# Q, K and V of batches 1 to 7 as three one-pass float32r products of 12-bit parts, made by GpSimd, in fills of 512 columns

## The chip, the cores and the metric

The kernel runs on one core of a Trainium2 chip. The metric is the device time of one execution in microseconds, the median of several runs. The engines are TensorE (PE in the profile, its weight loads PEld), VectorE (DVE), ScalarE (ACT), GpSimd (POOL) and SyncE (SP), which issues most of the DMAs.

## The reference, cut to what matters

The input x has 8 sequences ("batches" below) of 1,024 tokens and 256 features. One attention block with 16 heads of 16 dimensions is followed by two groups of a mixture of experts. Everything is float32.

```python
q = (x @ Wq.T + bq).reshape(B, L, H, Dh)
k = (x @ Wk.T + bk).reshape(B, L, H, Dh)
v = (x @ Wv.T + bv).reshape(B, L, H, Dh)
q = _rope(q, sin, cos)
k = _rope(k, sin, cos)
scores = jnp.einsum('bqhd,bkhd->bhqk', q, k) / jnp.sqrt(jnp.float32(Dh))
attn = jax.nn.softmax(scores, axis=-1)
out = jnp.einsum('bhqk,bkhd->bqhd', attn, v).reshape(B, L, D)
x = _layernorm(x + (out @ Wo.T + bo))
...
# two groups of 32 experts, top 2 of each, SwiGLU with 128 hidden units
x = _layernorm(x + moe(x))
```

The change touches the first three lines only (and where their results and the rotation's are kept).

## The kernel before

**Steps.** The attention of all eight batches is one software pipeline of 512 steps, 64 for a batch. A unit is four heads of a batch and takes 16 steps. In each step t TensorE does four score matmuls of 512 columns for the softmax maxima, 22 steps ahead (line 990, into two banks `ps_a` that VectorE reduces, two TENSOR_REDUCE a step on line 1242), four transposed score matmuls of 512 columns (line 980, into a ring of three banks `ps_b` that ScalarE turns into probabilities, four ACTIVATE a step on line 845), and the products of probabilities and V of step t-2 (line 1009, four heads side by side in the array). A score of line 990 and one of line 980 lie on different halves of the array's rows and go as a pair.

**Jobs.** Other work of TensorE is hung on steps by `schedule` and `chain_at`. For a batch that begins at step `start`, Q is computed in 8 steps and K in 8 (a block c of 128 output features and a quarter of 256 tokens each, line 908), and V in 8 (128 tokens each, line 918). They are float32 matmuls, two for a fill, one for each 128 input features. The steps of batch b carry the jobs for batch b+1. Counted from the start of a batch, Q and K stand in steps 8 to 15 and 31 to 38, and V in 57 to 63 and in step 0 of the next. The output projection of the batch before (O) has steps 22 to 29, the transposes (T) and the router (L) steps 48 to 53, the counts (R) step 14, and the rows of maxima (M) steps 12, 28, 44 and 60.

**Product with V, whole or halved.** It goes in two halves of 256 columns, between the score pairs, only where a step has no job:

```python
if in_a and 0 < (t - PV_LAG) % KC < KC - 1 and not b_jobs.get(t) and not a_jobs.get(t):
    pv(t - PV_LAG, k * HALF // 2, (k + 1) * HALF // 2)
elif k == 0:
    pv(t - PV_LAG, 0, HALF)
```

**VectorE's chores.** Layer norm, top 2, routing and ranks are cut into pieces that `between(t)` puts behind the reductions of a step, as far as a `room` reaches. In batches 0 to 6, room is 7 in a step with Q, K or V, 5 with O, and 0 in any other. Pieces of kind 0 (the split of the maxima, and `split_upper`, the masks that cut Q and K to their upper 12 bits) go out at their step whatever the room.

**GpSimd** works through `pool_order`: `split` (rotation of Q and K, six operations on 128 by 1,024 elements, then `lower`, two subtractions), `norm_o`, `choose`, `rank_sums`, and `list`, whose four scatters each wait for a given step of the product with V. SP sends out the parts of Q and K (`parts_out`), reads them back in stacked form (`stack`), and loads the next x (`next_x`) in one piece of 1 MB. All of these queues are in order. After the steps comes the expert stage, which the change leaves as it is but for a name.

## Time and profile before

| what | value |
|---|---|
| median of 3 runs | 2279.51 us (2279.37 to 2288.64) |
| span of the profiled execution | 2348.8 us |
| attention steps 0 to 63 (batch 0) | 182.8 us |
| attention steps 192 to 255 (batch 3) | 200.9 us |
| busy in batch 3: PE, DVE, ACT, POOL | 197.05, 177.88, 157.79, 92.82 us |
| first to last maximum of scores | 33.8 to 1611.4 us |

A step is read as the time from the start of its first TENSOR_REDUCE of line 1242 to that of the next step's; a batch has 128 of them. Busy times are sums over the stretch, and a busy TensorE isn't TensorE at its peak: the records overlap, so costs are taken from the starts of matmuls. The profiled execution is longer than the timed ones, so that differences are worked out against its own span.

### The profile page before, as it was taken

The page shows a single profiled execution, that of the slowest core. Times are in us where ns is not written, and L with a number is a line of the kernel's source. Part 1 is how long each engine was busy: PE and PEld are TensorE (multiplying, and loading weights), DVE is VectorE, ACT ScalarE, POOL GpSimd, SP SyncE. Part 2 cuts the span into 40 slices and gives each one's busy share as a digit, 9 for nine tenths or more (in the row PEclk, how much of TensorE's full clock was granted, in tenths as well). Part 3 has the DMA queues.
Part 4 walks back from the last instruction along what each step waited for, and adds up shares of the span by engine and source line. Part 5 has one row for each costly group of instructions (what it writes and reads, how often), then busy time and mean ns, then how long its engine had stood idle before and what let it go on. Part 6 is the DMA issues. An engine that isn't in the chain of part 4 may idle for free.

```text
span 2348.8 us, 46747 instructions
## 1 busy us (share of the span) xinstructions
PE 2205.4 (94%) x13885; PEld 1125.7 (48%) x13893; DVE 1774.4 (76%) x3301; ACT 1599.4 (68%) x3621; POOL 1037.2 (44%) x886
## 2 busy tenths in 40 slices
PE   8999999999999999999999999999888888999994
PEld 4433343433433343344344344333476666777773
...
GB/s 178 91 87 90 122 95 53 132 109 116 160 117 95 140 155 114 118 144 134 85 161 150 103 123 141 185 125 191 190 164 167 135 182 226 226 330 298 285 272 204
DMA packets 179667, 363.70 MB, mean 155 GB/s; under 512 B 31009, under 2 KB 113185, under 8 KB 175329
## 3 DMA queue, kind: packets, MB, share of 16 engines
...
## 4 chain that ended last, share of the span: by engine, by line
PE 78%; DVE 11%; issue 4%; ACT 2%; DMA 1%; another core or an unknown queue 1%; POOL 1%; SPq 1%; ACTq 0%; DVEq 0%; POOLq 0%
PE ps_a L990 24%; PE ps_o L1009 20%; PE ps_a L1797 7%; DVE maxima_sb L1242 7%; PE ps_b L908 5%; PE ps_b L1821 4%; PE ps_b L1797 3%; PE ps_b L980 3%; PE ps_b L918 3%; PE ps_a L1784 3%; PE ps_o L1821 2%; PE ps_b L1806 2%; ACT probs_sb L845 1%; PE ps_b L928 1%
## 5 line engine op out<-in xcount | busy, mean ns | idle before, releaser
L1242 DVE TENSOR_REDUCE maxima_sb<-ps_a 128x1 f32<-128x1024 f32 x1024 | 1233.8, 1220 | 184.1 <-PE ps_a L990 164.4
L845 ACT ACTIVATE probs_sb<-ps_b 128x512 f32<-128x512 f32 x2013 | 1087.2, 600 | 283.7 <-PE ps_b L980 244.3
L990 PE MATMUL ps_a<-k_stack_sb,q_stack_sb 48*128 48x512 f32 x2048 | 736.4, 444 | 25.6 <-DVE maxima_sb L1242 23.8
L980 PE MATMUL ps_b<-q_stack_sb,k_stack_sb 50*128 50x512 f32 x2013 | 745.3, 450 | 4.2 <-ACT probs_sb L845 2.6
L1009 PE MATMUL ps_o<-probs_sb,v_sb_sb 128*32 128x512 f32 (+1 forms) x5400 | 586.7, 507 | 0.7 <-ACT probs_sb L845 0.5
L990 PEld LDWEIGHTS ps_a<-k_stack_sb,q_stack_sb 48*128 48x128 f32 x2048 | 304.8, 185 | 552.5 <-issue 281.5
L1648 POOL DMA_INDIRECT y_dram<-y_rows_sb,spot_sb x318 | 313.5, 986 | 258.1 <-DVE y_rows_sb L2110 107.9
L174 POOL DMA_INDIRECT rows_dram<-stage_sb,listed_sb x208 | 202.6, 974 | 306.1 <-PE ps_o L1009 280.4
L980 PEld LDWEIGHTS ps_b<-q_stack_sb,k_stack_sb 50*128 50x128 f32 x2013 | 305.5, 186 | 47.5 <-ACT probs_sb L845 39.2
L1797 PE MATMUL ps_a<-w_gu_sb,x_cols_sb 128*128 x848 | 226.1, 390 | 4.5 <-ACT x_cols_sb L1704 2.8
L1009 PEld LDWEIGHTS ps_o<-probs_sb,v_sb_sb 128*32 128x32 f32 x5400 | 106.6, 108 | 236.1 <-issue 107.7
L414 POOL TENSOR_TENSOR feat_qk_sb<-feat_qk_sb,trig_sb 128x1024 f32<-128x1024 f32 x30 | 71.3, 2376 | 283.0 <-DMA swapped_sb<-feat_qk_sb 209.1
L1704 ACT ACTIVATE x_cols_sb<-ps_a 128x256 f32<-128x256 f32 x318 | 123.1, 388 | 99.4 <-PE ps_a L1784 49.1
L2101 DVE TENSOR_TENSOR spot_sb<-x_rows_sb,spare_sb 128x1 int32<-128x1 f32 x237 | 37.7, 159 | 175.9 <-ACT gate_sb L1710 108.3
L1797 PEld LDWEIGHTS ps_a<-w_gu_sb,x_cols_sb 128*128 128x128 f32 x848 | 149.1, 195 | 19.9 <-issue 7.2
L1821 PE MATMUL ps_b<-w_d_sb,hidden_t_sb 128*128 x416 | 135.0, 407 | 17.5 <-DVE y_rows_sb L2110 12.8
L1710 ACT ACTIVATE gate_sb<-ps_a 128x128 f32<-128x128 f32 x212 | 59.9, 283 | 123.4 <-PE ps_a L1797 69.1
L1784 PE MATMUL ps_a<-consts_sb,x_rows_sb 128*128 128x128 f32 x636 | 124.0, 277 | 3.6 <-DMA x_rows_sb<-rows_dram 3.6
L1806 PE MATMUL ps_b<-consts_sb,hidden_sb 128*128 128x128 f32 x318 | 89.5, 282 | 33.9 <-ACT hidden_t_sb L1755 16.8
L1797 PE MATMUL ps_b<-w_gu_sb,x_cols_sb 128*128 x424 | 111.6, 386 | 2.3 <-ACT x_cols_sb L1704 2.1
L1784 PEld LDWEIGHTS ps_a<-consts_sb,x_rows_sb 128*128 128x128 f32 x636 | 90.1, 143 | 39.9 <-issue 5.4
L808 ACT ACTIVATE feat_qk_sb<-ps_b,bias_sb 128x256 f32<-128x256 f32 x128 | 60.8, 475 | 68.1 <-PE ps_b L908 65.2
...
## 6 DMA issues: line engine op xcount, KB each, us to landing
...
```

The lines of the kernel that those rows point to most:

```text
L174: return pool.indirect_dma_start(dram["rows"][g], bass.IndirectOffsetOnAxis(ap=index, axis=0), source, None)
L845: act.activation(probs[t % NPR][:, j, :], src[:, :], ACT.Exp, scale=float(DH) ** -0.5).then_inc(s_bdrain, 1)
L980: pe.matmul(out[:, :], k_stack[u % NSTK][lo:lo + XROWS, jj, kc * P:(kc + 1) * P].bitcast(F32R), q_stack[u % NSTK][lo:lo + XROWS, jj, qh * ...
L990: ins = pe.matmul(out[:, kh, :], q_stack[u % NSTK][lo:lo + ROWS, jj, qt * P:(qt + 1) * P].bitcast(F32R), k_stack[u % NSTK][lo:lo + ROWS, j ...
L1009: ins = pe.matmul(ps_o[32 * j:32 * j + 32, lo:hi], v[:, at:at + 32], probs[t % NPR][:, j, lo:hi], start=kc == 0, stop=kc == KC - 1)
L1242: vec.tensor_reduce(maxima[u % 2][:, 1 - k, i:i + 1], src[:, :, :].rearrange("p a q -> p (a q)"), AX.X, ALU.max).then_inc(s_adrain, 1)
L1648: pool.indirect_dma_start(dram["y"][n // NT], bass.IndirectOffsetOnAxis(ap=spot[n % NSP][:, :], axis=0), y_rows[n % NY][:, :], None).then_ ...
L1704: act.activation(x_cols[n % NXT][:, :, :], ps_x[n % 2][:, 0:DC, :], ACT.Copy).then_inc(s_xc, 1)
L1784: ins = pe.transpose(ps_x[n % 2][:, dc, :], x_rows[n % NXG][:, dc * P:(dc + 1) * P], con("ident"))
L1797: ins = pe.matmul(ps_g[n % NGU][:, 0:2 * HID], x_cols[n % NXT][:, dc, :], w_gu[g][:, bass.ds(e * (DC * 2 * HID) + dc * 2 * HID, 2 * HID)], ...
L1806: pe.transpose(ps_h[:, 0:P], hidden[n % NGU][:, :], con("ident")).then_inc(s_ht, 1)
L1821: pe.matmul(y_bank(n)[:, 0:D], hidden_t[n % 2][:, :], w_d[:, bass.ds(e * D + down_at(g), D)], start=True, stop=True).then_inc(s_down, 1)
```

## The change

For batches 1 to 7, x and the weights are cut into an upper part, rounded by a copy into float32r, and a lower part, the rest. The product is then three float32r matmuls for each 128 input features: upper by upper, lower x by upper w, upper x by lower w. Q and K are filled 512 columns at a time, in four phases (block c, half h of the tokens), and V two blocks of 128 tokens at a time, so that 24 jobs become 12. In steps of the batch before they stand at 7, 9, 16, 18, 36, 38, 49 and 51 (Q and K) and at 40, 42, 58 and 62 (V). x arrives in halves of 512 KB, four loads for a batch, and GpSimd splits each (`x_split`). The masks of VectorE are gone; GpSimd makes both parts of Q and K (`part`, a copy and a subtraction). Q and K no longer have a tile of their own but lie in the lower part's place, so ScalarE waits for the parts of the block before to be out in DRAM before it writes them. The chain of norm, transposes and routing moves by some steps, ScalarE scales two blocks of rows a step in place of one, and VectorE's room is set anew.

```diff
+        else:
+            for c in range(DC):
+                for h in range(2):
+                    at = start + PHASE_AT[2 * c + h]
+                    put(b_jobs, at, "Q", b, c, h)
+                    put(b_jobs, at + 2, "K", b, c, h)
+                    if c == 1:
+                        for i, v in enumerate(V_AT[h]):
+                            put(b_jobs, start + v, "V", b, 2 * h + i)
...
-        at = dict(O=22, norm=23, scale=39, T=48, L=50, x1=48, top2=57, exp=67, route=73, choose=74, marks=75, R=78, ranks=79,
-                  rank_sums=80, choices=86)
+        at = dict(O=22, norm=23, scale=40, T=44, L=46, x1=44, top2=50, exp=73, route=74, choose=75, marks=76, R=78, ranks=79,
+                  rank_sums=80, choices=85)
...
+PRODUCTS = ((0, 0), (0, 1), (1, 0))
...
+PHASE_AT, V_AT = (-57, -48, -28, -15), ((-24, -22), (-6, -2))
+X_AT, X_SPLIT_AT = (-65.5, -54, -45, -21), (-61, -51, -37, -18)
...
-        k_step = lambda b, c: SPB * b + (-48, -16)[c]
-        pool_order = []
+        k_step = lambda b, c: SPB * b + ((-45, -12) if b else (-48, -16))[c]
...
+        def part(eng, b, c, which):
+
+            n = b * DC + c
+            at = pool_no[("split", (b, c))] + 6 + 2 * which
...
+            eng.wait_ge(s_pool, at)
+            eng.tensor_copy(parts[which][:, 0, :].bitcast(F32R), feat[which]).then_inc(s_pool, 1)
+            eng.wait_ge(s_pool, at + 1)
+            eng.tensor_tensor(feat[which], feat[which], parts[which][:, 0, :], ALU.subtract).then_inc(s_pool, 1)
+
+        def x_split(eng, b, phase):
+
+            n = x_no(b, phase)
+            eng.wait_ge(s_xt, 16 * (n + 1))
+            eng.tensor_copy(x_parts[:, 0], x_in).then_inc(s_xupper, 1)
+            eng.wait_ge(s_xupper, n + 1)
+            eng.tensor_tensor(x_parts[:, 1], x_in, x_parts[:, 0].bitcast(F32), ALU.subtract).then_inc(s_xlower, 1)
...
                 if q == 0 and (b, c) != (0, 0):
-                    wait_split(act, b * DC + c - 1)
...
+                    act.wait_ge(s_parts, 16 * 2 * (b * DC + c))
...
-                    i, n = t - at["scale"], 1 if at["rate"] == 1 else 4
+                    i, n = t - at["scale"], 2 if at["rate"] == 1 else 4
...
+            def features(which, b, c, h):
+                out = b_tile()
+                pe.wait_ge(s_wparts, 2)
+                pe.wait_ge(s_xlower, x_no(b, 2 * c + h) + 1)
+                for n, (dc, w, x) in enumerate((dc, w, x) for dc in range(DC) for w, x in PRODUCTS):
+                    ins = pe.matmul(out[:, :], (w_upper, w_lower)[w][:, which, dc, c * P:(c + 1) * P],
+                                    x_parts[:, x, dc, :], start=n == 0, stop=n == DC * len(PRODUCTS) - 1)
+                ins.then_inc(s_bfill, 1)
+
+            def values(b, i):
+                out = b_tile()
+                pe.wait_ge(s_xlower, x_no(b, 2 + i // 2) + 1)
+                for a in range(2):
...
-                        chores += [(at, 0, split_upper(b, c, 0)), (at + 3, 0, split_upper(b, c, 1))]
...
+                    room[0] = min(room[0], 0) + 6
+                elif any(name in held for name in "QKV"):
+                    room[0] = min(room[0], 0) + 14
                 else:
-                    room = 7 if any(name in held for name in "QKV") else 0
+                    room[0] = min(room[0], 0) + (5 if "T" in held else 2)
```

On TensorE, in the steps before a batch begins, a V fill (`ps_b<-w_v_sb,x_t_sb`) has two matmuls. Before:

```order
L990 MATMUL ps_a<-k_stack_sb,q_stack_sb 128x512
L980 MATMUL ps_b<-q_stack_sb,k_stack_sb 128x512
L918 MATMUL ps_b<-w_v_sb,x_t_sb 128x256 x2
L990 MATMUL ps_a<-k_stack_sb,q_stack_sb 128x512
L980 MATMUL ps_b<-q_stack_sb,k_stack_sb 128x512
```

Now, for batch 1, lines 1068 and 1058 being the former 990 and 980:

```order
L1068 MATMUL ps_a<-k_stack_sb,q_stack_sb 128x512
L1058 MATMUL ps_b<-q_stack_sb,k_stack_sb 128x512
L996 MATMUL ps_b<-w_upper_sb,x_parts_sb 128x256 x2
L996 MATMUL ps_b<-w_lower_sb,x_parts_sb 128x256
L996 MATMUL ps_b<-w_upper_sb,x_parts_sb 128x256 x2
L996 MATMUL ps_b<-w_lower_sb,x_parts_sb 128x256
L996 MATMUL ps_b<-w_upper_sb,x_parts_sb 128x256 x2
L996 MATMUL ps_b<-w_lower_sb,x_parts_sb 128x256
L996 MATMUL ps_b<-w_upper_sb,x_parts_sb 128x256 x2
L996 MATMUL ps_b<-w_lower_sb,x_parts_sb 128x256
L1068 MATMUL ps_a<-k_stack_sb,q_stack_sb 128x512
```

Twelve matmuls for 256 tokens stand where two stood for 128. A fill of Q or K is six matmuls of 512 columns in the same way.

On GpSimd, early in a batch's steps, between `norm_o` (`o_feat_sb`) and `rank_sums` (`totals_sb`), before:

```order
L468 TENSOR_TENSOR o_feat_sb<-o_feat_sb,o_den_sb 128x1024
L470 TENSOR_SCALAR o_feat_sb<-o_feat_sb,bias_sb 128x1024
L497 TENSOR_TENSOR totals_sb<-incl_sb,totals_sb 128x512
L499 TENSOR_TENSOR totals_sb<-totals_sb,counts_sb 128x512
```

and now:

```order
L514 TENSOR_TENSOR o_feat_sb<-o_feat_sb,o_den_sb 128x1024
L516 TENSOR_SCALAR o_feat_sb<-o_feat_sb,bias_sb 128x1024
L477 CAST x_parts_sb<-x_t_sb 128x1024
L479 TENSOR_TENSOR x_parts_sb<-x_t_sb,x_parts_sb 128x1024
L543 TENSOR_TENSOR totals_sb<-incl_sb,totals_sb 128x512
L545 TENSOR_TENSOR totals_sb<-totals_sb,counts_sb 128x512
```

The second half of x is split behind `norm_o`, and TensorE needs it in step 16.

On VectorE, around steps 8 to 15 of a batch (`maxima_sb` the reductions, two a step), the same pieces stand in both programs; before they lie in steps that hold Q or K, now only step 9 does. Now:

```order
L1320 TENSOR_REDUCE maxima_sb<-ps_a 128x1 x2
L1177 RECIPROCAL den_sb<-den_sb 128x128
L1320 TENSOR_REDUCE maxima_sb<-ps_a 128x1 x4
L1168 TENSOR_SCALAR max_parts_sb<-maxima_sb 128x2x16
L1171 TENSOR_TENSOR max_parts_sb<-maxima_sb,max_parts_sb 128x2x16
L1217 TENSOR_REDUCE denom_sb<-shifted_sb 128x16
L1220 RECIPROCAL denom_sb<-denom_sb 128x16
L1320 TENSOR_REDUCE maxima_sb<-ps_a 128x1 x4
L1227 TENSOR_TENSOR hot_sb<-consts_sb,expert_sb 128x512 x2
L1320 TENSOR_REDUCE maxima_sb<-ps_a 128x1 x4
L1156 COPY totals_sb<-ps_a 128x2x8x32
L1158 COPY logits_sb<-ps_a 128x512
```

A count of x4 is two steps without a chore between them.

## Rows read from the trace of the kernel before

**Rows 1.** The page: busy time of the engines, and the chain of waits by engine

```profile
PE 2205.4 (94%) x13885; PEld 1125.7 (48%) x13893; DVE 1774.4 (76%) x3301; ACT 1599.4 (68%) x3621; POOL 1037.2 (44%) x886
...
PE 78%; DVE 11%; issue 4%; ACT 2%; DMA 1%; another core or an unknown queue 1%; POOL 1%; SPq 1%; ACTq 0%; DVEq 0%; POOLq 0%
```

**Rows 2.** Busy time by stretch, batch 0 and batch 3

```profile
core 0: us, PE busy (x) PEld busy (x) DVE busy (x) ACT busy (x) POOL busy (x), PEclk, DMA share, GB/s
88.80:271.70 182.90, 181.46 (x1336) 71.62 (x1338) 157.91 (x141) 151.85 (x292) 42.42 (x17) 1.00 0.40 97
672.60:873.50 200.90, 197.05 (x1363) 81.50 (x1360) 177.88 (x244) 157.79 (x306) 92.82 (x71) 1.00 0.47 128
```

**Rows 3.** Timeline of PE, half of a step without a job

```profile
686.04 0.64 PE L1009 MATMUL ps_o<-probs_sb,v_sb_sb 128*32 128x256 f32 x8
686.61 0.50 PE L990 MATMUL ps_a<-k_stack_sb,q_stack_sb 48*128 48x512 f32 x1
...
686.94 0.39 PE L990 MATMUL ps_a<-k_stack_sb,q_stack_sb 48*128 48x512 f32 x1
...
687.27 0.64 PE L1009 MATMUL ps_o<-probs_sb,v_sb_sb 128*32 128x256 f32 x8
```

**Rows 4.** Timeline of PE around a Q job (start, length)

```profile
778.43 1.13 PE L908 MATMUL ps_b<-x_t_sb,w_q_sb 128*128 128x256 f32 x4
779.49 0.50 PE L990 MATMUL ps_a<-k_stack_sb,q_stack_sb 48*128 48x512 f32 x1
...
779.83 0.39 PE L990 MATMUL ps_a<-k_stack_sb,q_stack_sb 48*128 48x512 f32 x1
...
780.16 1.07 PE L1009 MATMUL ps_o<-probs_sb,v_sb_sb 128*32 128x512 f32 x8
781.15 0.50 PE L990 MATMUL ps_a<-k_stack_sb,q_stack_sb 48*128 48x512 f32 x1
```

**Rows 5.** Timeline of weight loads, the same Q job

```profile
778.43 0.73 PEld L908 LDWEIGHTS ps_b<-x_t_sb,w_q_sb 128*128 128x128 f32 x4 [0.36 <-issue]
```

**Rows 6.** The chain of waits in order of time, a router job of 64 columns

```profile
426.47 0.84 PE ps_a L952 x8
```

**Rows 7.** Busy by stretch: steps 8-15 and 16-21 of batch 3, 8-15 of batch 7

```profile
693.50:722.90 29.40, 28.99 (x174) 12.28 (x177) 24.85 (x28) 22.27 (x44) 11.25 (x8) 1.00 0.32 85
722.90:737.60 14.70, 14.45 (x124) 5.14 (x126) 14.12 (x13) 12.54 (x25) 13.68 (x9) 1.00 0.60 111
...
1500.90:1525.30 24.40, 21.53 (x174) 7.42 (x170) 24.15 (x27) 18.75 (x36) 11.88 (x9) 1.00 0.53 160
```

**Rows 8.** Timeline of DVE, a step without a job and with a chore

```profile
1505.07 0.68 DVE L1139 TENSOR_REDUCE denom_sb<-shifted_sb 128x16 f32<-128x512 f32 x1
1505.66 2.35 DVE L1242 TENSOR_REDUCE maxima_sb<-ps_a 128x1 f32<-128x1024 f32 x2
1507.92 0.17 DVE L1086 TENSOR_SCALAR max_parts_sb<-maxima_sb 128x32 int32<-128x32 int32 x1
```

**Rows 9.** Busy by stretch, the masks of line 439 alone, batch 3

```profile
672.60:873.50 200.90, 3.50 (x4) 1.00 0.47 128
```

**Rows 10.** Timeline of POOL: last scatter before norm_o, norm_o, rank_sums

```profile
688.22 0.97 POOL L174 DMA_INDIRECT rows_dram<-stage_sb,listed_sb  x1 [1.49 <-PE ps_o L1009]
...
708.65 2.37 POOL L468 TENSOR_TENSOR o_feat_sb<-o_feat_sb,o_den_sb 128x1024 f32<-128x1024 f32 x1 [6.97 <-DMA o_den_sb<-inv_dram]
...
716.42 2.85 POOL L470 TENSOR_SCALAR o_feat_sb<-o_feat_sb,bias_sb 128x1024 f32<-128x1024 f32 x1
```

**Rows 11.** Groups by line and form, POOL (busy us, mean ns)

```profile
L747 POOL MEMSET v_sb_sb<- 128x2192 f32 x1 | 1.9, 1930 | 0.1
```

**Rows 12.** Timeline of ACT, a step in which it also scales a block

```profile
799.15 0.60 ACT L869 ACTIVATE y_sb<-y_sb,shift_sb,rstd_sb 128x256 f32<-128x256 f32 x1
799.65 2.08 ACT L845 ACTIVATE probs_sb<-ps_b 128x512 f32<-128x512 f32 x4
801.62 0.60 ACT L869 ACTIVATE y_sb<-y_sb,shift_sb,rstd_sb 128x256 f32<-128x256 f32 x1
```

**Rows 13.** Timeline of SP: rows for the lists, parts out, stacks in

```profile
772.38 0.36 SPq L672 DMA_DIRECT2D stage_sb<-x_dram  x1
772.84 0.41 SPq L586 DMA_DIRECT2D parts_dram<-parts_k_sb  x1
778.52 1.79 SPq L610 DMA_DIRECT2D q_stack_sb<-parts_dram  x4
```

More of the change, by code:

```diff
@@ L386, in program @@
             pool_no[(name, args)] = count
-            count += {"split": SPLIT_STEPS if args != (0, 0) else 0, "bias_y": 1, "norm_o": 2 * DC, "choose": 0, "rank_sums": 0, "list": 0}[name]
+            count += {"split": SPLIT_STEPS if args != (0, 0) else 0, "bias_y": 1, "norm_o": 2 * DC, "choose": 0, "rank_sums": 0, "list": 0,
+                      "x_parts": 0, "w_parts": 0}[name]
         norm_o_done = lambda b: pool_no[("norm_o", (b,))] + 2 * DC
@@ L410, in rotate @@
             f = feat[which]
-            eng.wait_ge(s_bdrain, b_no[("QK"[which], b, c, QUARTERS - 1)] + 1)
+            eng.wait_ge(s_bdrain, b_no[("QK"[which], b, c, pieces(b) - 1)] + 1)
             wait_swapped(eng, b, c, which)
@@ L417, in rotate @@
             eng.tensor_tensor(f[:, :], f[:, :], swapped, ALU.add).then_inc(s_pool, 1)
-        def lower(eng, b, c, which):
+        def part(eng, b, c, which):
             n = b * DC + c
-            eng.wait_ge(s_mask, 2 * n + which + 1)
-            if n:
-                eng.wait_ge(s_parts, 16 * 2 * n)
+            at = pool_no[("split", (b, c))] + 6 + 2 * which
+            if which == 0 and c == 1 and b >= 2:
+                eng.wait_ge(s_afill, a_no[("L", b - 2, KC // 2 - 1)] + 1)
+            eng.wait_ge(s_parts, 16 * 2 * n)
@@ L559, in swap @@
             def swap(b, c, which):
-                sp.wait_ge(s_bdrain, b_no[("QK"[which], b, c, QUARTERS - 1)] + 1)
+                sp.wait_ge(s_bdrain, b_no[("QK"[which], b, c, pieces(b) - 1)] + 1)
                 if which == 1:
@@ L761, in attention_gpsimd @@
                     rotate(pool, *args, 1)
-                    lower(pool, *args, 0)
-                    lower(pool, *args, 1)
+                    part(pool, *args, 0)
+                    part(pool, *args, 1)
+                elif name == "x_parts":
+                    x_split(pool, *args)
+                elif name == "w_parts":
+                    w_split(pool)
                 elif name == "bias_y":
@@ L951, in route @@
                     for dc in range(DC):
-                        ins = pe.matmul(out[:, 0, a * NG * NE:(a + 1) * NG * NE], x1_of(b)[:, 2 * i + a, dc, :], router[:, dc, :],
+                        ins = pe.matmul(out[:, 0, a * NG * NE:(a + 1) * NG * NE], x1_of(b, 2 * i + a)[:, dc, :], router[:, dc, :],
                                         start=dc == 0, stop=dc == DC - 1)
@@ L1091, in split_max @@
                 yield 2
-            def split_upper(b, c, which):
-                upper(vec, b, c, which)
-                yield 4
             def recip(b):
@@ L1193, in attention_vector @@
                     at = chain_at(nb, b)
[L1194 to L1195 removed]
+                    chores += [(end + 8, 0, recip(b)), (at["norm"], 2, norm(b)), (at["top2"], 3, top2(b)), (at["route"], 0, route(b)),
+                               (at["marks"], 0, marks(b)), (at["ranks"], 0, ranks(b)), (at["choices"], 0, ranks_of_choices(b))]
             chores.append((chain_at(nb, nb - 2)["table"], 7, early_table()))
+            room = [0]
             def between(t):
```

148 lines of the change are left out of this document (88 added, 60 removed).

## The prediction

> **What bounds the kernel now.** I read the page first. TensorE is busy 94% of the span and holds 78% of the chain of waits, with VectorE at 11% [rows 1]. A busy TensorE says little by itself, so I went to the stretches. A batch from the second on costs some 200 us: in batch 3 TensorE is busy 197.05 of 200.9 us, VectorE 177.88, ScalarE 157.79, GpSimd 92.82, all at a granted clock of 1.00, the 2.4 GHz level; batch 0 is shorter and has little of VectorE's chores [rows 2]. Then the timeline, to price a step by the starts of its matmuls. In a step without a job two pairs of scores take 0.33 us each and half the product with V 0.57 us (686.04 to 686.61 to 686.94 to 687.27), in all 1.23 us a half and 2.46 a step [rows 3]. With a job, the product with V is whole and takes 0.99 us (780.16 to 781.15), and the pairs 4 x 0.33, which makes 2.31 us, and the job adds 778.43 to 779.49, 1.06 us: 3.37 us in all [rows 4]. VectorE is close behind: two reductions back to back take 2.26 us (1505.66 to 1507.92) of those 2.46 [rows 8], so a step without a job has 0.2 us for chores and one with a job 1.1. ScalarE fills a step to the end once it also scales a block: 801.62 - 799.15 = 2.47 us for five instructions, 0.49 each [rows 12]. The reader should see three engines within 10% of each other in the empty steps. TensorE work that is saved in a batch moves time only as far as the other two let it.
>
> **TensorE's part.** Removed are 24 job steps of a batch at 3.37 us, 80.9 us. Added are 12 job steps, and 12 become empty at 2.46 us, 29.5 us (an empty step is dearer than 2.31 since its product with V is halved). The price of a new job isn't in the trace. The old job has four records, each 256 columns in two passes, 512 clocks, and its weight loads lie behind the matmul ahead, as four loads spread over 0.73 us show [rows 5]. Four times 0.213 us leaves 0.21 us for entry and exit of 1.06. A float32r matmul of 512 columns in one pass is again 512 clocks, so six give 6 x 0.213 + 0.21 = 1.49 us. The bound above is that each one pays what a pair of scores pays, 0.33 us [rows 3], that is 1.98. I take 1.49, since the shape is that of the old job: full array, no switch of tiles. For V, twelve matmuls of 256 columns are 12 x 0.107 + 0.21 = 1.49 us if the load of 128 columns hides. The router's eight loads come 0.84/8 = 0.105 us apart [rows 6], just as long as such a matmul, so it is close; in series they would give 12 x 0.212 = 2.5. I take 1.59. New sum: 8 x 3.80 + 4 x 3.90 + 29.5 = 75.5 us, so **-5.4 us a batch**; at the upper bounds (+3.9 and +3.6) it would be +2.1.
>
> The Trainium skill, "TensorE: Matmul & The Clock Gate", section "Back-to-back issue gap", gives about 131 ns for a sustained matmul of 512 columns in a real kernel. By it, as an estimate, a Q or K job would be 1.0 us and the change worth 27 us more over seven batches. The rows here don't agree: no quarter of the job of 1.06 us can be that short, and I leave it out of the sum.
>
> **VectorE's part.** The masks go, 3.50 us a batch [rows 9]. Two lay in O steps and two in V steps, partly covered; I take **-1.0**. But the chores stay, and half of the steps with room for them lose their job. The last batch shows what that costs, since it has the same chores and no projections: its steps 8 to 15 take 24.4 us with VectorE busy 24.15, against 29.4 in batch 3 [rows 7]. The K job in step 9 adds some 0.9 of its 1.34 us, so 25.3, a saving of 4.1 where TensorE's price alone (seven steps at -0.91, one at +0.43) says 5.9: **+1.8** back. In step 21, now an empty one, stand two reductions of the kind on line 1139 (0.68 us each [rows 8]) and a small one, 1.5 us; with 0.2 us of room a step and a bank of lag, **+0.8**. The single small pieces that the new room of 2 lets into empty steps fit in the 0.2.
>
> **ScalarE.** In steps 40 to 43 it has 16 probabilities, 8 scalings, 2 V drains and a copy of o, 27 x 0.49 = 13.2 us, where TensorE has 2 x 3.90 + 2 x 2.46 = 12.7. **+0.3**, as the old scaling steps had a part of this too. Larger drains (8 of 512 for 16 of 256) save ScalarE time that nobody waits for.
>
> **GpSimd.** Four x splits and the copies of `part` are new: eight copies and four subtractions of 1,024 elements. The subtraction is 2.37 us as other two-input operations are [rows 10]. A copy lies between the memset, 1.93 us for 2,192 elements or 0.9 for 1,024 [rows 11], and the operation with a scalar, 2.85 us [rows 10]; I take 1.1, since a copy has no arithmetic. Together 18 us on a queue that is busy 93 of 201 us: not a bound, but it is in order and TensorE now waits for it. First split: the last scatter ends at 689.2, 16.6 us into the batch [rows 10], or 15.8 by the new step times; 3.6 us more is 19.4, and TensorE comes to the Q of step 7 at 7 x 2.46 + 2.31 = 19.5. No wait. Second: `norm_o` ends at 719.27 [rows 10], 46.7 us in, and the split 50.3. TensorE gets to step 16's job at 17.2 + 3.8 + 25.3 + 2.3 = 48.6: it waits, **+1.5**. A wait here holds up all that is queued behind on TensorE, so both other engines starve. At 2.85 a copy these waits would be 1.7 and 3.5 us, +3.7 for the batch. The fourth split, ahead of step 49, has two steps of cover, some 6 us for 4.6.
>
> The Trainium skill, "GPSIMD Engine Reference", section "4.1 Engine selection", would leave elementwise work with VectorE, GpSimd being about twice as slow on two inputs and about line rate on one. For the subtraction the trace agrees (2.37 us); for the copy it would mean an estimate of 0.9 us, and a sum lower by 0.2 us a wait.
>
> **DMA.** The x halves carry the bytes of before. `parts_out` of the first block now stands on SP behind the rows for the third list, whose wait for a scatter ended at 772.38, 99.8 us in [rows 13]. One step later is 102.3. Both parts then go out together; 1 MB alone needed 5.7 us before the stack could be issued (772.84 to 778.52), two may need up to 11.4. They land 108.7 to 114.4 us in, and ScalarE, which now waits for them before it writes Q, gets there at about 114. Cost nothing, just.
>
> **Sum.** -5.4 - 1.0 + 1.8 + 0.8 + 0.3 + 1.5 = -2.0 us a batch. Six batches (1 to 6): -12. Batch 0 has neither O nor ranks, so -5.4 and -0.8 for its masks: -6.2. Batch 7 loses the V of its step 0, -0.9. In all -19 us: 2348.8 becomes 2330 in the profiled execution. The timed runs have a median 69 us below that span; attention ran at full clock in the profile, so I put the same 19 us on the median: **2260 us**.
>
> **Rivals.**
> 1. Half of TensorE's gain eaten, as worked out: 2248 to 2268, chance 0.50.
> 2. TensorE's whole gain arrives, because the lag of banks covers the chores and GpSimd is early: 7 x -6.4 = -45, 2235. For it: VectorE has 23 us a batch to spare. Against: steps 8 to 15 of the last batch. Chance 0.12.
> 3. All of it is eaten, by VectorE's chores and the second split with a dear copy: -2.0 + 2.2 = about 0 a batch, -5 in all, 2274. Chance 0.24.
> 4. Slower, by one mechanism: the parts of the first block land late and ScalarE stands in step 36 with the probabilities queued behind it, so that the three banks fill and TensorE stops. It costs each us beyond 114. From 5 us late on, in six batches, the kernel is slower than before by over 0.5%; at 8 us it is 2279.5 - 19 + 48 = 2308. For it: the order on SP and a margin of about nothing. Against: 5.7 us for 1 MB. Chance 0.11. Weight loads in series and pairs' price (+7.5 a batch, 2312) have 0.03.
>
> **How the numbers follow.** The likeliest is the first, its own range 2248 to 2268. The range for 8 in 10 takes in most of 2 and 3: 2238 to 2284. About 0.5%, 11 us, is what a measurement of this kernel can tell from no change. Faster by more: the first two, 0.62; within: the third, 0.24; slower: the fourth and the series of loads, 0.14.
>
> **What would show it.** A Q fill should take 1.5 us from its first matmul to the next score, a V fill 1.5 to 1.7; steps 8 to 15 of a middle batch about 25 us; a wait of TensorE for GpSimd's lower x ahead of the second Q fill, 1 to 2 us a batch, and none ahead of the others; the cast on GpSimd 0.9 to 1.5 us; batch 0 about 176.5 us and batch 3 about 199. I am wrong if float32r pays more than a pass, if the cast costs over 2 us, or if ScalarE waits for the parts' DMA.

## The result and the profile after

The changed kernel takes **2341.06 us** (median of 4 runs, 2326.39 to 2350.82); the kernel before, on the same chip, 2279.44 us (2278.08 to 2288.64). The ratio is 1.0247, 95% interval 1.0191 to 1.0303: slower by 2.5%. I had forecast 2260, with 0.62 on faster. Comparisons leave disturbed runs out, so a ratio can differ a little from that of two medians.

The page of the changed kernel, busy time by engine and the chain by engine:

```profile
PE 2199.2 (94%) x14349; PEld 1143.9 (49%) x14357; DVE 1775.5 (76%) x3271; ACT 1580.9 (67%) x3537; POOL 1171.8 (50%) x974
...
PE 70%; DVE 14%; issue 4%; POOL 3%; ACT 3%; DMA 3%; SPq 2%; ACTq 0%; DVEq 0%; POOLq 0%
```

Against [rows 1] TensorE's busy time hardly moved, and its share of the chain fell from 78 to 70%: what came in its place is VectorE, GpSimd and transfers. VectorE lost its masks and has the same busy time, 1775.5 for 1774.4. That is the first sign that something else in it grew.

Busy time by stretch: 33 to 120 us, batch 0, batches 1 to 6 together, batch 3, and its steps 8 to 15 and 16 to 21 (us, then PE, PEld, DVE, ACT, POOL busy with counts, the granted clock, DMA):

```profile
33.00:120.00 87.00, 86.74 (x215) 43.80 (x213) 59.71 (x53) 14.45 (x31) 28.63 (x14) 0.51 0.36 96
108.60:295.00 186.40, 183.23 (x1404) 74.84 (x1406) 158.03 (x136) 148.33 (x281) 65.07 (x31) 0.96 0.39 88
295.00:1552.10 1257.10, 1190.55 (x8548) 501.22 (x8556) 1065.39 (x1406) 928.40 (x1758) 621.33 (x441) 0.98 0.47 124
710.20:915.70 205.50, 194.33 (x1427) 82.24 (x1426) 176.75 (x239) 154.72 (x294) 112.01 (x84) 1.00 0.49 131
731.90:759.30 27.40, 24.22 (x182) 9.03 (x178) 25.60 (x26) 19.83 (x38) 13.95 (x10) 1.00 0.31 93
759.30:779.90 20.60, 18.07 (x134) 7.33 (x132) 16.37 (x17) 15.04 (x28) 11.22 (x9) 1.00 0.62 126
```

Batch 3 against [rows 2]: TensorE's busy time fell by 2.7 us, as it should, but the batch grew by 4.6, so TensorE stands idle 11.2 us where it stood 3.9. Steps 8 to 15 take 27.4 us against 29.4 [rows 7]; I had said 25.3. The clock is the 2.4 GHz level all through batch 3. In the stretch from 33 to 120 us it is at half, with TensorE busy without a gap, and 0.98 over batches 1 to 6.

The kernel before, profiled once more (e4), gives the yardstick that the first profile could not: its stretch behind the last maximum of the scores is 669 us, where the first profile had 739. The same stretches of it (33 to 120 us, batches 1 to 6, batch 3):

```profile
33.00:120.00 87.00, 83.02 (x376) 38.32 (x377) 77.61 (x70) 31.29 (x63) 18.74 (x8) 0.96 0.41 110
...
274.50:1481.80 1207.30, 1182.72 (x8157) 489.77 (x8164) 1063.18 (x1443) 946.13 (x1830) 510.01 (x369) 1.00 0.46 123
677.30:878.10 200.80, 196.99 (x1363) 81.62 (x1360) 177.72 (x243) 157.68 (x306) 92.69 (x71) 1.00 0.46 128
```

The spans differ by 2349.0 - 2274.8 = 74.2 us. Of these 49.8 are in batches 1 to 6 (1257.1 - 1207.3), 17.8 ahead of step 0 (108.6 against 90.8), 2.6 in batch 0, 4 behind. So there are two questions: what costs 8.3 us a batch, and what halves the clock in the prelude.

**The jobs cost what I had said.** Timeline of PE, the Q fill in step 7 of batch 3, the first of batch 4's projections:

```profile
729.54 0.70 PE L986 MATMUL ps_b<-x_parts_sb,w_upper_sb 128*128 128x512 f32 x2
730.08 0.40 PE L986 MATMUL ps_b<-x_parts_sb,w_lower_sb 128*128 128x512 f32 x1
730.31 0.62 PE L986 MATMUL ps_b<-x_parts_sb,w_upper_sb 128*128 128x512 f32 x2
730.77 0.40 PE L986 MATMUL ps_b<-x_parts_sb,w_lower_sb 128*128 128x512 f32 x1
731.10 0.50 PE L1068 MATMUL ps_a<-k_stack_sb,q_stack_sb 48*128 48x512 f32 x1
```

731.10 - 729.54 = 1.56 us (predicted 1.49); a V fill took 1.62 (1.59). The Q fill of step 16 had to wait first:

```profile
761.69 0.70 PE L986 MATMUL ps_b<-x_parts_sb,w_upper_sb 128*128 128x512 f32 x2 [2.16 <-POOL x_parts_sb L479]
```

**What I had not looked for** stands in the timelines of DVE and POOL around step 12 of batch 3, first DVE:

```profile
747.01 2.43 DVE L1227 TENSOR_TENSOR hot_sb<-consts_sb,expert_sb 128x512 bf16<-128x512 f32 x2
749.36 2.34 DVE L1320 TENSOR_REDUCE maxima_sb<-ps_a 128x1 f32<-128x1024 f32 x2
...
758.02 1.38 DVE L1237 TENSOR_TENSOR_SCAN incl_sb<-scan_bf_sb,totals_sb 128x512 f32<-128x512 bf16 x1
```

and POOL:

```profile
745.88 2.40 POOL L514 TENSOR_TENSOR o_feat_sb<-o_feat_sb,o_den_sb 128x1024 f32<-128x1024 f32 x1 [2.58 <-DMA o_den_sb<-inv_dram]
748.38 3.69 POOL L516 TENSOR_SCALAR o_feat_sb<-o_feat_sb,bias_sb 128x1024 f32<-128x1024 f32 x1
752.05 2.36 POOL L514 TENSOR_TENSOR o_feat_sb<-o_feat_sb,o_den_sb 128x1024 f32<-128x1024 f32 x1
754.50 2.84 POOL L516 TENSOR_SCALAR o_feat_sb<-o_feat_sb,bias_sb 128x1024 f32<-128x1024 f32 x1
757.29 1.03 POOL L477 CAST x_parts_sb<-x_t_sb 128x1024 fp32r<-128x1024 f32 x1
758.41 3.13 POOL L479 TENSOR_TENSOR x_parts_sb<-x_t_sb,x_parts_sb 128x1024 fp32r<-128x1024 f32 x1
```

The two one-hot tables take 2.43 us, where the kernel before needs 1.36. The first of them takes 1.82 us for 0.68 and ends at 748.83, 0.55 us behind GpSimd's operation (748.28). GpSimd's next one, begun at 748.38 beside the rest of the tables, takes 3.69 instead of 2.85. Each engine pays for the other. At 758.41 the split of x meets the scan, and takes 3.13 us instead of 2.38. The maxima, which read PSUM and run through all of this, keep their 1.22.

One line's instructions in batches 1 to 6, of before (e4) (min/median/max in ns): the split of the maxima, the tables, the scan, the list positions

```profile
L1086 DVE TENSOR_SCALAR max_parts_sb<-maxima_sb x24: 170/171/172, 305.1 to 1463.6; 128x32 int32<-128x32 int32 x24
L1149 DVE TENSOR_TENSOR hot_sb<-consts_sb,expert_sb x10: 680/682/685, 507.6 to 1315.4; 128x512 bf16<-128x512 f32 x10
L1159 DVE TENSOR_TENSOR_SCAN incl_sb<-scan_bf_sb,totals_sb x5: 1197/1202/1225, 522.9 to 1330.1; 128x512 f32<-128x512 bf16 x5
L1181 DVE SCALAR_TENSOR_TENSOR listed_sb<-expert_sb,rank_sb x5: 176/178/180, 551.8 to 1357.8; 128x32 int32<-128x32 f32 x5
```

and of the changed kernel, with the maxima as a control:

```profile
L1168 DVE TENSOR_SCALAR max_parts_sb<-maxima_sb x24: 170/174/2384, 325.8 to 1536.0; 128x32 int32<-128x32 int32 x24
L1227 DVE TENSOR_TENSOR hot_sb<-consts_sb,expert_sb x10: 677/1248/2854, 536.9 to 1375.7; 128x512 bf16<-128x512 f32 x10
L1237 DVE TENSOR_TENSOR_SCAN incl_sb<-scan_bf_sb,totals_sb x5: 1384/2439/2524, 547.9 to 1386.3; 128x512 f32<-128x512 bf16 x5
L1259 DVE SCALAR_TENSOR_TENSOR listed_sb<-expert_sb,rank_sb x5: 561/775/820, 570.6 to 1405.9; 128x32 int32<-128x32 f32 x5
L1320 DVE TENSOR_REDUCE maxima_sb<-ps_a x770: 1159/1224/1227, 293.8 to 1552.1; 128x1 f32<-128x1024 f32 x193
```

The same code, up to 14 times as long in its worst instance. The Trainium skill names this: "SBUF — State Buffer", section "SBUF: two separate sides", says that VectorE in a two-port mode, or with two inputs in SBUF (against a GpSimd instruction that reads SBUF), and GpSimd take one pair of ports as an exclusive lock for a whole instruction, and the other waits; the trace agrees (2384 ns for 170).

Call an instruction's duration less the shortest of the same form in that trace its stretched time. Summed over VectorE's instructions that lost over 0.1 us, reductions left out (they vary by 0.07 us with or without GpSimd), it is 26.1 us in batches 1 to 6, against 6.2 before. To it come TensorE's waits for the lower x parts, 9.9 us in four (5.38 in batch 1, 2.17 and 2.16 in batches 2 and 3, and 0.15), and the clock: 58.0 us of batches 1 to 6 at the 1.2 GHz level against 3.4, in pieces of 3.4 to 10.2 us, which begin during or just behind a wait of TensorE for the one or the other (batch 3, all at 2.4 GHz, was an exception).

### The profile page after: what moved, and what is told of

It reads as the page before. It is cut to its first block, busy times and chain, and to the rows that moved or that the text cites. A ratio compares the mean times of both kernels' runs of the same rounds, so it can differ in the third digit from the quotient of the medians.

```text
span 2349.0 us, 47558 instructions
## 1 busy us (share of the span) xinstructions
PE 2199.2 (94%) x14349; PEld 1143.9 (49%) x14357; DVE 1775.5 (76%) x3271; ACT 1580.9 (67%) x3537; POOL 1171.8 (50%) x974
## 3 DMA queue, kind: packets, MB, share of 16 engines
q10 hardware_dynamic: 1464, 2.38, 0.4%
## 4 chain that ended last, share of the span: by engine, by line
PE 70%; DVE 14%; issue 4%; POOL 3%; ACT 3%; DMA 3%; SPq 2%; ACTq 0%; DVEq 0%; POOLq 0%
PE ps_a L1068 20%; PE ps_o L1087 18%; DVE maxima_sb L1320 8%; PE ps_a L1875 6%; PE ps_b L1899 3%; PE ps_b L1875 3%; PE ps_b L986 3%; PE ps_b L1058 3%; PE ps_a L1862 2%; PE ps_o L1899 2%; PE ps_b L996 2%; ACT probs_sb L906 1%; PE ps_b L1884 1%; PE ps_b L967 1%; SPq L577 1%
## 5 line engine op out<-in xcount | busy, mean ns | idle before, releaser
L1068 PE MATMUL ps_a<-k_stack_sb,q_stack_sb 48*128 48x512 f32 x2048 | 746.1, 460 | 46.6 <-DVE maxima_sb L1320 42.2
L1058 PE MATMUL ps_b<-q_stack_sb,k_stack_sb 50*128 50x512 f32 x2013 | 762.1, 456 | 8.2 <-ACT probs_sb L906 6.1
L1087 PE MATMUL ps_o<-probs_sb,v_sb_sb 128*32 128x256 f32 (+1 forms) x5864 | 604.3, 484 | 1.1 <-ACT probs_sb L906 0.5
L1068 PEld LDWEIGHTS ps_a<-k_stack_sb,q_stack_sb 48*128 48x128 f32 x2048 | 315.8, 193 | 555.8 <-DVE maxima_sb L1320 404.6
L1058 PEld LDWEIGHTS ps_b<-q_stack_sb,k_stack_sb 50*128 50x128 f32 x2013 | 311.1, 188 | 65.9 <-ACT probs_sb L906 58.5
L1087 PEld LDWEIGHTS ps_o<-probs_sb,v_sb_sb 128*32 128x32 f32 x5864 | 115.9, 108 | 256.9 <-issue 168.0
L1875 PE MATMUL ps_a<-w_gu_sb,x_cols_sb 128*128 x848 | 221.2, 384 | 0.7 <-ACT x_cols_sb L1782 0.7
L1899 PE MATMUL ps_b<-w_d_sb,hidden_t_sb 128*128 x416 | 129.8, 394 | 8.6 <-DVE y_rows_sb L2188 5.4
L454 POOL TENSOR_TENSOR parts_q_sb<-parts_q_sb,trig_sb 128x1024 f32<-128x1024 f32 x15 | 35.7, 2378 | 177.1 <-DMA swapped_sb<-parts_q_sb 177.0
L1833 ACT ACTIVATE hidden_t_sb<-ps_b 128x128 f32<-128x128 f32 x318 | 88.0, 277 | 4.7 <-PE ps_b L1884 4.5
```

Source lines behind the costliest of these rows:

```text
L1058: pe.matmul(out[:, :], k_stack[u % NSTK][lo:lo + XROWS, jj, kc * P:(kc + 1) * P].bitcast(F32R), q_stack[u % NSTK][lo:lo + XROWS, jj, qh * ...
L1068: ins = pe.matmul(out[:, kh, :], q_stack[u % NSTK][lo:lo + ROWS, jj, qt * P:(qt + 1) * P].bitcast(F32R), k_stack[u % NSTK][lo:lo + ROWS, j ...
L1087: ins = pe.matmul(ps_o[32 * j:32 * j + 32, lo:hi], v[:, at:at + 32], probs[t % NPR][:, j, lo:hi], start=kc == 0, stop=kc == KC - 1)
L1875: ins = pe.matmul(ps_g[n % NGU][:, 0:2 * HID], x_cols[n % NXT][:, dc, :], w_gu[g][:, bass.ds(e * (DC * 2 * HID) + dc * 2 * HID, 2 * HID)], ...
L1899: pe.matmul(y_bank(n)[:, 0:D], hidden_t[n % 2][:, :], w_d[:, bass.ds(e * D + down_at(g), D)], start=True, stop=True).then_inc(s_down, 1)
```

## The experiments

All twelve in one table. "Batches 1-6" is the length of that stretch in the windows view (its ends are the first maximum of step 0 of batches 1 and 7); "low" is the time in it at the 1.2 GHz level; "stretched" is worked out as above. All in us.

| kernel | median | ratio to before (95%) | batches 1-6 | low | stretched |
|---|---|---|---|---|---|
| before again (e4) | 2276.7 (one run) | | 1207.3 | 3.4 | 6.2 |
| changed | 2341.06 | 1.0247 (1.0191-1.0303) | 1257.1 | 58.0 | 26.1 |
| e1 more unread | 2337.86 | 1.0247 (1.0162-1.0332) | 1247.1 | 37.5 | 24.6 |
| e2 256 columns | 2354.35 | 1.0325 (1.0273-1.0376) | 1268.2 | 85.3 | 32.2 |
| e3 plain float32 | 2350.69 | 1.0286 (1.0238-1.0334) | 1257.5 | 37.5 | 21.1 |
| e5 x early | 2307.89 | 1.0090 (1.0053-1.0127) | 1222.2 | 17.1 | 16.1 |
| e6 and tables alone | 2302.42 | 1.0098 (1.0056-1.0140) | 1222.4 | 20.5 | 14.9 |
| e7 fills over chores | 2348.76 | 1.0259 (1.0176-1.0343) | 1261.0 | 71.7 | 28.1 |
| e8 parts on GpSimd only | 2315.22 | 1.0122 (1.0072-1.0171) | 1238.6 | 47.8 | 28.1 |
| e9 e6 and three waits | 2302.50 | 1.0055 (1.0020-1.0090) | 1220.2 | 17.1 | 8.1 |
| e10 e8 and one wait | 2278.14 | 0.9984 (0.9946-1.0023) | 1204.6 | 0 | 6.9 |
| e12 e9, a wait moved | 2289.62 | 1.0021 (0.9982-1.0059) | 1210.9 | 10.2 | 1.5 |
| e11 e12, scaling spread | 2277.33 | 0.9977 (0.9937-1.0016) | 1199.3 | 0 | 0.6 |

### e1 and e4: is it the clock of the prelude?

```diff
-UNREAD = 19
+UNREAD = 21
```

> The changed kernel with 21 instead of 19 of the unread matmuls of the prelude, nothing else. Theory A (the clock of the first 120 us): in the changed kernel's profile TensorE waits 1.8 us for the first stack behind the last unread matmul, and the granted clock is 0.5 from 33.5 us for 85 us; two more unread matmuls at 0.4 us each fill half of that wait, so the low stretch should be gone and the time should fall by about 20 us, to 2321. Rival: the fall of the clock has another cause than this gap; then the stretch from 33.5 us stays and the time stays at 2341.

> The kernel before, profiled once more. Its first profile had a span of 2349 us though its timed runs took 2279, and its stretch behind the last attention step (1610 us on) took 739 us against 670 in the changed kernel. If that is a matter of the one execution, this profile has a tail near 670 us, and a span near 2280; if it belongs to every profiled execution, it is 739 us again.

In e1 TensorE goes into the first score without the gap of 1.8 us, and the clock falls all the same, 5 us later (38.5 us on, for 78.5), with no gain in time. Theory A falls. Later profiles settle more: e6 and e12, with the whole change in them, kept the clock up over most of the prelude (step 0 at 90.0 and 89.8 us), e6 even behind a gap of 2.36 us, and so did e10 behind one of 2.48. e8, whose prelude differs from that of before in a copy for a mask, did not.

The runs of the kernel before form two groups: of the 23 timed beside e11 and e12, 12 take 2268.98 to 2286.93 us at a mean granted clock of 0.982 to 0.990, and 11 take 2289.82 to 2300.90 at 0.969 to 0.976. The means of the groups differ by 18 us, as much as the fall cost in the prelude (17.8). So the fall of the prelude's clock seems to happen to the kernel before as well (inferred: neither of its two profiles caught one), and the change isn't needed for it. Whether the change makes it more frequent stays open.

It bears on the size of the loss: the four runs of before beside the changed kernel (2278.08 to 2288.64) look like the first group, while the changed kernel's profile has the fall; its fastest run, 2326.39, is 47 us above the median before. e4 shows that the 739 us tail was a matter of one execution.

### e2 and e3: fill size, and the price of the products

e2 gives each phase four fills of 256 columns, in 24 steps; e3 keeps the 12 fills and takes the parts away.

```diff
# e2
-                    put(b_jobs, at, "Q", b, c, h)
-                    put(b_jobs, at + 2, "K", b, c, h)
+                    for i in range(2):
+                        put(b_jobs, at + i, "Q", b, c, 2 * h + i)
+                        put(b_jobs, at + 2 + i, "K", b, c, 2 * h + i)
...
# e3
-                for n, (dc, w, x) in enumerate((dc, w, x) for dc in range(DC) for w, x in PRODUCTS):
+                for dc in range(DC):
+                    ins = pe.matmul(out[:, :], (w_q, w_k)[which][:, dc, c * P:(c + 1) * P], x_in[:, dc, :],
...
```

> The changed kernel with the size of a fill undone: 24 fills of 256 columns a batch (8 for each of Q, K, V) in 24 steps, still of three float32r products of the parts that GpSimd makes. The steps between them are given to VectorE's chores as before the change (8 a step). Theory B (VectorE's chores lie bare, since 12 of the 24 steps that covered them are now empty): the steps with a fill are about 3.2 us instead of 3.37 before and cover the chores again, so a batch is about 200 us instead of 205 to 215, and the time about 2290 or less. Rival C (the extra work on GpSimd, or the wait for its x parts, is what costs): little changes, 2325 to 2345.

> The changed kernel with its 12 fills of 512 columns a batch in their 12 steps, but of plain float32 matmuls (2 a fill) straight from x; GpSimd splits neither x nor the weights. A fill should take about 1.9 us instead of 1.56. Theory B (chores bare in empty steps): the 12 jobs cost 12 x 0.35 = 4 us more a batch, the wait for GpSimd's x parts (2 us in the batch looked at) goes, so about 2341 + 7 x 2 = 2355 us. Rival C (GpSimd's splits and what they hold up are the loss): a batch is 3 us or more shorter in spite of the longer fills, 2320 or less.

e2 is slower still. The fills are short (a step of 3.22 us), and there are 24 steps to cover chores again, yet nothing comes back. This isn't a clean test of theory B, since three other things grew: the stretched time (32.2) and the low clock (85.3), the highest of all, and a new wait. With Q of the second block in step 37, ScalarE waits there for the parts' transfer (19.4 us in batches 2 to 6), and TensorE behind it for 11.5:

```profile
ACT parts_q_sb L869 <- DMA parts_dram<-parts_k_sb: 19.4, 5, 6.9
PE ps_b L1060 <- ACT parts_q_sb L869: 11.5, 5, 5.3
```

(us in total, times, longest.) That is the mechanism of my rival 4. e3 meets the number of theory B, 2351 for 2355, but says little by it: longer fills raised TensorE's work, and the stretched time fell only from 26.1 to 21.1. The copies of `part` and the later placement were still there, which I take for the reason; no run separates them.

### e5 and e6: GpSimd's order in steps 11 to 15

```diff
-X_AT, X_SPLIT_AT = (-65.5, -54, -45, -21), (-61, -51, -37, -18)
+X_AT, X_SPLIT_AT = (-65.5, -54.9, -45, -21), (-61, -52.75, -37, -18)
-                pool_order.append((SPB * (b + 1) + 11, "norm_o", (b,)))
+                pool_order.append((SPB * (b + 1) + 11.5, "norm_o", (b,)))
# e6 also, in norm_o
+            if 1 <= b < nb - 1:
+                eng.wait_ge(s_route, ROUTE_STEPS * b)
```

> The changed kernel with the second split of x on GpSimd ahead of the normalisation of the attention output instead of behind it (its load one step earlier), nothing else. Theory D (TensorE's wait for x parts is 2.2 us of the 5 to 6 us that a batch is longer than before): the wait of the second Q fill goes, an undisturbed batch is 203.8 us instead of 206.0, and the time about 15 us lower, 2325. Rival: the wait was hidden behind VectorE's chores in the same steps, so something else is late next (the ranks at step 14 to 21), a batch stays at 206 and the time at 2340.

> The kernel of e5 with, in addition, a wait of GpSimd's normalisation until VectorE has made its two one-hot tables at step 12. Theory E (VectorE's operations with two SBUF inputs, or narrow copies from SBUF to SBUF, don't start or don't end while GpSimd runs an operation: in the changed kernel the two tables take 2.6 us or more instead of 1.37, the scan 2.0 instead of 1.2, the splits of the maxima up to 2.4 instead of 0.17, 28 us in all over seven batches against 6 before the change): here the two tables run beside the x split at worst, step 12 is about 1 us shorter than in e5, and the sum of such stretched time falls from 28 us to about 20. Rival: the stretched rows are not on TensorE's path; then the rows get shorter and the batch doesn't.

e5 takes 33 us off the median, twice the 15 that I expected. TensorE's waits for x parts fall from 9.9 to 0.3 us; with them go 10 us of stretched time (the tables and the scan no longer meet anything long) and 41 us of low clock. A wait costs more than its length when the clock falls behind it. Batch 3 itself moved only from 205.5 to 205.0, with a low piece of 3.4 us in it. I had expected e6 to make step 12 a microsecond shorter than in e5. That was a miss: step 12 of batch 3 is 3.78 us in e6 and 3.79 in e5 (4.93 in the changed kernel), so the earlier split had already kept GpSimd off the tables. The list positions of step 21 and the splits of step 26 stay stretched in both (steps of 4.50 and 5.14 us in e6), and batches 1 to 6 stay at 1222: no gain over e5 that these runs can tell.

### e7: fills over the longest chores

```diff
-PHASE_AT, V_AT = (-57, -48, -28, -15), ((-24, -22), (-6, -2))
-X_AT, X_SPLIT_AT = (-65.5, -54, -45, -21), (-61, -51, -37, -18)
+PHASE_AT, K_AFTER, V_AT = (-57, -47, -27, -15), (5, 4, 2, 2), ((-23, -21), (-6, -2))
+X_AT, X_SPLIT_AT = (-65.5, -51.9, -42.5, -20.5), (-61, -51, -35, -18)
...
```

> The changed kernel with four of the twelve fills moved so that they stand in the steps with VectorE's longest chores (K of the first half to step 12, beside the one-hot tables; Q and K of the second half to steps 17 and 21, beside the rank reductions), what hangs on them a step or three later, and a little more room for chores in the other steps. Theory B (in a step without a fill VectorE's own two maxima, 2 x 1.22 us, are as long as the step, so that each chore there is bare, and in a step with a fill up to 1.5 us of chores is covered): steps 12 and 21 together are 9.3 us in the changed kernel and about 2.5 us of that falls away, 15 us over the program, to 2325. Rival: what is taken off there comes back as a wait for x parts at step 17 or for the parts at step 37, 2340 or more.

A miss. Step 12 took 6.00 us in batches 2, 3 and 5, its tables stretched by 2.21, and 4.23 in batch 4, where they weren't. At step 33 a split of x now met VectorE's Newton chain (the inverse root of layer norm) and stretched it by 2.7 us. The rival that I had named came true as well: with Q of the second block in step 37, ScalarE waited for the parts, and TensorE for ScalarE, batches 1 to 6:

```profile
ACT parts_q_sb L868 <- DMA parts_dram<-parts_k_sb: 22.0, 5, 8.0
PE ps_b L1058 <- ACT parts_q_sb L868: 13.5, 4, 6.3
```

The x waits fell from 9.9 to 3.0 us in return. To move a fill moves GpSimd and the transfers behind it, so this run doesn't settle theory B either.

### e8 and e10: one part of the change, and one wait

e8 is the kernel before, with `upper` on GpSimd as a copy to float32r. e10 adds one wait ahead of the addition of the bias to y.

```diff
# e8
-                    lower(pool, *args, 0)
-                    lower(pool, *args, 1)
+                    for which in range(2):
+                        upper(pool, *args, which)
+                        lower(pool, *args, which)
...
-                        chores += [(at, 0, split_upper(b, c, 0)), (at + 3, 0, split_upper(b, c, 1))]
# e10 also
                     pool.wait_ge(s_y, 16 * (b + 1))
+                    if b < nb - 1:
+                        pool.wait_ge(s_max, MAX_STEPS * (UPB * (b + 1) + 1))
```

> The kernel before with only one part of the change: GpSimd makes the upper parts of Q and K (a copy to float32r, 1.04 us) instead of VectorE (a mask, 0.68 us, four a batch); fills, x and placement as before. Theory E (GpSimd and VectorE hold each other up): the four masks of 0.68 to 2.7 us go from VectorE, which by themselves cost before at most 6 us over the program in stretched time; GpSimd's rows move little, so the time is 2270 to 2280: this part alone is not what made the kernel slower. Rival: the 1.04 us copies behind each rotation stretch VectorE's other rows or delay the stacks, 2290 or more.

> The kernel of e8 (before, with only the upper parts of Q and K made on GpSimd) with one wait more: GpSimd's addition of the bias to y (4.57 us) waits until VectorE has split the maxima at step 58. In e8 that split waited 3.9 us for the addition in each batch, step 58 took 7.40 us instead of 3.28, and the clock fell behind it. Theory E: step 58 is 3.3 us again, the clock stays up in steps 60 to 62, a batch is 200 us or less, and the time 2270 to 2280. Rival: the 4.1 us go elsewhere (another row of VectorE meets the later addition), and the time stays at 2300 or more.

My number for e8 was wrong, and its rival right: 2315. Timeline of DVE in e8, step 58 of batch 3:

```profile
881.24 1.23 DVE L1238 TENSOR_REDUCE maxima_sb<-ps_a 128x1 f32<-128x1024 f32 x1 [0.36 <-PE ps_a L990]
882.38 4.06 DVE L1086 TENSOR_SCALAR max_parts_sb<-maxima_sb 128x32 int32<-128x32 int32 x1
886.48 0.19 DVE L1089 TENSOR_TENSOR max_parts_sb<-maxima_sb,max_parts_sb 128x32 f32<-128x32 f32 x1
```

and of POOL:

```profile
879.52 2.38 POOL L427 TENSOR_TENSOR parts_k_sb<-feat_qk_sb,parts_k_sb 128x1024 f32<-128x1024 f32 x1
881.86 4.54 POOL L767 TENSOR_TENSOR y_sb<-y_sb,bo_row_sb 128x2048 f32<-128x2048 f32 x1
```

32 numbers a partition, 0.17 us of work, wait for an addition of 4.54 us that began 0.5 us earlier and that nobody needs for 28 steps. Both are old instructions; what was moved only made GpSimd's chain late enough for them to meet. Step 58 takes 7.40 us, and behind it the clock falls (PEclk, the column before the last two):

```profile
882.00:889.30 7.30, 4.62 (x30) 1.88 (x32) 7.27 (x10) 3.48 (x8) 4.54 (x2) 1.00 0.00 0
889.30:896.00 6.70, 6.70 (x25) 2.50 (x21) 5.20 (x28) 3.34 (x8) 0.00 (x0) 0.50 0.03 6
```

With the wait, DVE in e10:

```profile
857.29 0.17 DVE L1088 TENSOR_SCALAR max_parts_sb<-maxima_sb 128x32 int32<-128x32 int32 x1
857.49 0.19 DVE L1091 TENSOR_TENSOR max_parts_sb<-maxima_sb,max_parts_sb 128x32 f32<-128x32 f32 x1
```

and POOL:

```profile
857.83 4.56 POOL L769 TENSOR_TENSOR y_sb<-y_sb,bo_row_sb 128x2048 f32<-128x2048 f32 x1 [1.05 <-DVE max_parts_sb L1091]
```

Step 58 is 3.51 us again. One wait of 1.05 us on GpSimd takes 34 us off batches 1 to 6 (1238.6 to 1204.6) and 37 off the median, no low clock is left there, and the kernel is level with before. This is the cleanest proof: nothing else differs between the two. It is of a part of the change only; for the whole, see e12.

### e9, e12 and e11: the changed kernel with its engines kept apart

```diff
# e9, in rotate and part
+            if b >= 3 and c == 0 and which == 0:
+                eng.wait_ge(s_rank, RANK_STEPS * (b - 2))
+            if b and c == 1 and which == 1:
+                eng.wait_ge(s_max, MAX_STEPS * (UPB * b + 1))
+            if b and c == 0 and which == 0:
+                eng.wait_ge(s_max, MAX_STEPS * (UPB * (b - 1) + 3))
...
# e12: the last one moved from part into rotate, for which == 1
# e11
-        at = dict(O=22, norm=23, scale=40, T=44, L=46, x1=44, top2=50, ...
...
-                    i, n = t - at["scale"], 2 if at["rate"] == 1 else 4
+        at = dict(O=22, norm=23, scale=37, T=45, L=47, x1=45, top2=51, ...
...
+                    i, n = t - at["scale"], 1 if at["rate"] == 1 else 4
```

> The kernel of e6 (x split early, tables beside nothing of GpSimd's) with three more waits of GpSimd, so that VectorE's other operations with SBUF on both sides run alone too: the rotation of the first half waits for the list positions of step 21, one subtraction waits for the split of the maxima of step 26, one addition of the rotation for that of step 58. Theory E (GpSimd and VectorE hold each other up, and the stretched rows are on TensorE's path): in e6 these rows are stretched by 18 us over seven batches, of which nearly all goes; steps 21, 26 and 58 shrink by 0.7, 1.3 and 0.5 us, a batch is 202 us or less instead of 204.7, and the time 2280 to 2288. Rival: GpSimd's chain, 3 us later, delays the stacks or the x parts of step 36 and gives it back: 2300 or more.

e9 was half a miss. Steps 21 and 58 of batch 3 shrank (3.78 and 3.74 us), but with GpSimd later, ScalarE waited 4.86 us for the parts in batch 6 and TensorE 3.24, as the rival has it, and another of GpSimd's additions met the split at step 26 (batch 3), the DVE timeline of which reads:

```profile
781.04 0.17 DVE L1176 TENSOR_SCALAR max_parts_sb<-maxima_sb 128x32 int32<-128x32 int32 x1
781.24 2.40 DVE L1179 TENSOR_TENSOR max_parts_sb<-maxima_sb,max_parts_sb 128x32 f32<-128x32 f32 x1
```

The first row got through before that addition began at 781.23, the second did not.

> The kernel of e9 with one of its three waits moved: in e9 the subtraction that waited for the split of the maxima at step 26 came too late, and another addition of the rotation (2.37 us) met that split instead: its second row took 2.40 us, and step 26 5.94 instead of 3.71. Now that addition waits for the split. Theory E: step 26 is 3.7 us, a batch is 200.5 instead of 202.7, and the time about 15 us lower than e9's. Rival: GpSimd, now 5 us later there, holds up the x parts for step 36, where a wait for GpSimd appears, and the time is e9's.

> The kernel of e12 with the second thing taken off that the trace of e9 shows: ScalarE scales two rows of y a step in steps 40 to 43, beside the V drains of steps 40 and 42, and TensorE waits for its probabilities there (0.5 us at a time; the four steps take 14.9 us). Here it scales one row a step from step 37 to 44, and the transposes, logits and the second store follow one step later. Theory F (ScalarE bounds steps 40 to 43): the four steps take about 13.2 us, a batch is about 1.5 us shorter than in e12, the time about 10 us less. Rival: the scaling at step 37 waits for the end of VectorE's Newton chain and holds up the probabilities of step 37 or 38: no gain.

In e12 step 26 is 4.01 us for 5.94, the waits for x parts sum to 0.3 us, and the median is 13 us lower. Batches 1 to 5 average 200.8 us, those of before 201.3; batch 6 takes 206.9, where ScalarE waits 2.99 us for the parts and 10.2 us of low clock follow. In e11 steps 40 to 43 take 13.6 us for 14.9, and batches 1 to 6 1199.3, the shortest of all, 8 us under before. Over the whole program e11 is level with before: 2277.33 against 2286.93 in medians, but a ratio of 0.9977 whose interval holds 1. Medians say little where runs fall into two groups: those at a mean clock above 0.98 average 2275.3 (7 of e11) and 2277.6 us (12 of before). Of the 8 us, e11's profile gives 3.2 back in batch 0 and 2.6 behind batch 6. I have no version that is shown to beat the kernel before.

## Why the prediction was wrong

- **TensorE's part, -5.4 us a batch: right in price.** 1.56 and 1.62 us a fill for 1.49 and 1.59, by which the part is -4.7. With them TensorE's busy time fell 2.7 us in batch 3 (its records count a halved product with V as more).
- **VectorE's part, masks -1.0 and chores +1.8: the step that failed.** I priced each chore with its duration in the kernel before, as if a duration belonged to the instruction. It belongs to the pair of engines. The sign lay in a row that I used: the four masks of 3.50 us [rows 9] are three of 0.68 and one of 1.46, which met GpSimd. VectorE's pieces grew by 20 us in batches 1 to 6, 3.3 a batch, where the sum had 1.8 for being uncovered and nothing for this. A batch was to get 2.0 us shorter and got 8.3 longer (49.8 over six).
- **GpSimd, "not a bound": right as to its load, and wrong in what follows.** It was 112 of 205 us busy. A queue far from full still lengthens another engine's instructions. The copy at 1.03 us was as priced (1.1). The second x wait, predicted +1.5, was 2.17 and 2.16 in batches 2 and 3, and 5.38 in batch 1; in batches 4 to 6 it was 0.15 or nothing. A sum over equal batches had neither.
- **The clock had no term.** I wrote that attention ran at full clock, of the kernel before. 54.6 us more at half speed are worth at most 27 us. e1 against the changed kernel says 10 us for 20.5 us of it, with x waits equal in sum and stretched time within 1.5; by that rate it is some 26, an estimate. Stretched time (19.9), x waits (9.9) and this make 56 for a loss of 49.8 and a small gain on TensorE. The three overlap, so this is no exact split.
- **ScalarE, +0.3 in steps 40 to 43: mis-sized.** The four steps took 14.9 us where the sum had 13.0; spreading the scaling took 1.3 us off them (13.6).
- **Step 21, +0.8:** 3.78 us where it ran alone (e9), 1.3 over an empty step.
- **Rival 4** (late parts, ScalarE waiting in step 36) was the one I had for slower. In the changed kernel ScalarE waited for the parts in none of batches 1 to 6, and the transfer cost nothing. The sign was rival 4's, the cause wasn't. But the margin was as thin as the prediction has it: once something was moved the wait appeared, 19.4 us in e2, 22.0 in e7, 4.9 in e9, 4.0 in e12 and 5.2 in e11.
- **Batch 0**, forecast at 176.5 us, took 186.4. The prelude's low clock reaches into it (to 118.8 us; step 0 is at 108.6), and a split of 0.19 us took 2.29. Without that low clock it was still 183.6 in e12, with the same 2.29 in it, against 183.8 before: the gain of 6.2 didn't come, and the rest of it isn't explained.
- With the cause taken away and the scaling spread (e11), the six batches gain 8 us where I had 12. That looks near, but e11 has neither the x wait (+1.5) nor the +0.3, so the same sum promises it -3.8 a batch, some 23 in all. About 15 us of TensorE's gain are still lost. In batch 3 steps 8 to 15 take 26.2 us (25.3 in the sum), step 21 3.78 (3.26) and steps 40 to 43 13.6 (12.7), which is 2.3 of it; why stays open.
